# Two rounding steps taken out of the activation quantisers, Gelu released per tile, the offset of 129 moved into a column-sum bias, and no barrier between the blocks of the second feed-forward matmul

## What is computed

```python
x = x + attention(layernorm(x))
x = x + ffn(layernorm(x), w1, w2)

def _quant_weight(w):                       # ternary
    s = clip(mean(abs(w)), EPS, None)
    return clip(round(w / s), -1.0, 1.0) * s

def _quant_act(x):                          # whole numbers -128..127 per row
    scale = 127.0 / clip(max(abs(x), axis=-1, keepdims=True), EPS, None)
    return clip(round(x * scale), -128.0, 127.0) / scale

def ffn(x, w1, w2):
    h = gelu(quant_act(x) @ quant_weight(w1).T)      # 1024 -> 4096
    return quant_act(h) @ quant_weight(w2).T         # 4096 -> 1024
```

## Time and profile before

| what | us |
|---|---|
| median of 2 runs | 9029.53 (9015.09 to 9043.97) |
| profiled execution, its own time | 9021.79 |
| its span, slowest core (core 7) | 9020.3 |
| spans of the 8 cores | 8992.3 to 9020.3 |
| DVE busy | 3543.7 (39% of the span) |
| PE busy | 3752.3 (42%) |
| ACT busy | 1939.5 (22%) |
| transfers, mean over the span | 42 GB/s |

### The profile page before, as it was taken

One profiled execution on the slowest core, in us unless ns is written; L12 is line 12 of the kernel. 1 busy time (PEld: TensorE's weight loads), 2 busy tenths in 40 slices (PEclk: granted clock), 3 DMA queues, 4 the chain that ended last, 5 costly groups with the idle time before them and its releaser, 6 DMA issues.

```text
span 9020.3 us, 46886 instructions; the slowest of 8 cores (8992.3 to 9020.3 us)
## 1 busy us (share of the span) xinstructions
PE 3752.3 (42%) x13056; PEld 1408.0 (16%) x13056; DVE 3543.7 (39%) x4302; ACT 1939.5 (22%) x2197; POOL 0.2 (0%) x4
## 2 busy tenths in 40 slices
PE   3225465666653555666652003221333033025445
PEld 0000211222221211222221001110111011012222
DVE  0341323333322223333313776557555665740000
ACT  1012202555531302555421110000000000001111
POOL 0000000000000000000000000000000000000000
PEclk8666665777765755777755556655666566567778
DMA  4233100000002000000011001110111001122221
GB/s 151 98 118 96 33 0 1 9 8 10 8 26 70 21 0 3 9 9 9 9 42 49 28 31 40 56 47 10 56 56 56 27 29 56 56 63 70 75 75 54
DMA packets 204263, 374.90 MB, mean 42 GB/s; under 512 B 24345, under 2 KB 155806, under 8 KB 199922
## 3 DMA queue, kind: packets, MB, share of 16 engines
q1 hardware_dynamic: 204018, 371.92, 12.7%
HBM read 296.07 MB, written 75.76 MB: 41 GB/s over the span
## 4 chain that ended last, share of the span: by engine, by line
DVE 36%; PE 32%; ACT 15%; issue 6%; DMA 6%; SPq 3%; DVEq 1%; ACTq 0%
ACT pslab L786 8%; PE ps_F L1274 5%; DVE rlrow L830 5%; PE ps_F L1150 5%; PE pss L274 3%; PE ps_S L812 2%; PE ps_W L900 2%; PE ps_qn L760 2%; PE ps_FM L798 2%; DVE hflt L1202 2%; DVE hflt L1198 2%; DVE hflt L1200 2%; DVE htile L1197 2%; PE ps_mu L618 2%; DVE colmisc L1181 2%
## 5 line engine op out<-in xcount | busy, mean ns | idle before, releaser
L786 ACT ACTIVATE pslab<-ps_S 128x1024 bf16<-128x1024 f32 x1024 | 979.6, 1022 | 277.7 <-PE ps_S L812 275.7
L830 DVE RECIPROCAL rlrow<-ps_FM 1x512 f32<-1x512 f32 x128 | 429.0, 3352 | 1158.3 <-PE ps_FM L798 1151.3
L812 PE MATMUL ps_S<-qt,kt 65*128 65x512 bf16 x2048 | 713.6, 440 | 158.0 <-ACT pslab L786 122.5
L1213 PE MATMUL ps_trH<-s_idb,hqtm 128*128 128x128 bf16 x1024 | 129.4, 306 | 1540.8 <-DVE colmisc L1206 1439.3
L798 PE MATMUL ps_FM<-pslab,vaug 128*65 128x512 bf16 x2048 | 684.6, 422 | 170.3 <-DVE aostg L834 147.9
L1274 PE MATMUL ps_F<-hqin,w2tb 128*128 128x512 bf16 x2048 | 488.4, 400 | 556.2 <-DMA hqin<-scr_hq 337.3
L274 PE MATMUL pss<-wab,s_onescolf 128*1 128x512 f32 x512 | 310.2, 756 | 558.7 <-ACT wab L254 419.9
L1150 PE MATMUL ps_F<-w1tb,yi_fm 128*128 128x512 bf16 x2048 | 459.7, 387 | 180.0 <-DMA w1tb<-scr_w1t 179.3
L1174 ACT ACT_TABLE_LOAD x32 | 41.1, 1283 | 2120.2 <-DVE hqfm L1221 1134.7
L760 PE MATMUL ps_qn<-qsq,s_bo 128*65 128x512 f32 x256 | 233.4, 1012 | 373.3 <-DVE qt L768 323.4
L1163 DVE TENSOR_SCALAR htile<-ps_F,c1c 128x512 f32<-128x512 f32 x256 | 192.2, 751 | 447.8 <-PE ps_F L1150 436.6
(11 more groups left out here) (186 smaller groups left out, 4803.9 us busy)
## 6 DMA issues: line engine op xcount, KB each, us to landing
w1tb<-scr_w1t SPq DMA_DIRECT2D x512, 128.0 KB, 2.7
wst<-w1t SPq DMA_DIRECT2D x24, 2048.0 KB, 9.5
wst<-w2t SPq DMA_DIRECT2D x96, 512.0 KB, 3.8
xstage<-x SPq DMA_DIRECT2D x64, 512.0 KB, 4.1
scr_hq<-hqfm SPq DMA_DIRECT2D x256, 128.0 KB, 1.9
hqin<-scr_hq SPq DMA_DIRECT2D x256, 128.0 KB
rlb<-scr_rl SPq DMA_DIRECT2D x64, 256.0 KB, 3.4
scr_x<-x2asm SPq DMA_DIRECT2D x32, 512.0 KB, 2.8
```

Of the source, the lines that this page charges most:

```text
L786: sE.inc(q.activation(out=pslab[:, 1024 * (gl % 4):1024 * (gl % 4 + 1)], in_=psS[kt % 2][:], func=AF.Exp))
L812: ins = q.matmul(out=psS[kt % 2][:, 512 * s:512 * (s + 1)], lhsT=kt65[:, N * g + 128 * kt: N * g + 128 * (kt + 1)], rhs=qt65[hb][:, 1024 * ...
L830: VS(q, q.reciprocal(out=rlrow[0:1, 1024 * ph + 512 * s:1024 * ph + 512 * (s + 1)], in_=psFM[64:65, 512 * s:512 * (s + 1)]))
L1213: ins = q.transpose(out=pstr[:, 128 * j:128 * (j + 1)], in_=hqtm[:, 128 * hc:128 * (hc + 1)], identity=idb[:])
```

## The change

It makes five edits.

1. In `ln3_quant_phase` the comparison with 1.5 is gone (one DVE instruction of 128 x 1024 per tile).
2. In `ffn1_phase` the comparison with 1.5 is gone too, and the comparison with -0.5 writes straight to the bf16 tile `hqtm`, so the subtraction of 129 is gone: `hqtm` now holds values that are 129 too large.
3. For these 129, `ffn2_phase` gets a new step after `w_tern`: 256 matmuls with `w2tb` as the stationary and a column of ones as the moving operand give the column sums of `w2tb` in PSUM (`psCS`, 128 x 8). DVE multiplies them by -129 into `w2cs`. The copy of line 1284 becomes an Identity activation with `w2cs[:, dc]` as its bias. A barrier follows the new step.
4. The Gelu of tile `tt` waits only for the last `ps_F` scaling of its own tile (`bv + 4 * 7 + tt + 1`).
5. The barrier after each block of `ffn2_phase` goes; one remains after the last block. Waits take its place: SP waits for the previous block's PE steps before it loads `hqin`, and for the previous block's DVE steps before it loads `xst`; DVE waits for the stores of `y` before it writes `oasm`; PE waits for ACT and DVE from the first chunk on.

```diff
--- before.py
+++ after.py
@@ -1082,8 +1082,6 @@
                                       op=OP.subtract))
                 VS(q, q.scalar_tensor_tensor(out=yjunk[:, 0:D], in0=ytmp[:], scalar=0.5,
                                              in1=yjunk[:, 0:D], op0=OP.is_gt, op1=OP.add))
-                VS(q, q.scalar_tensor_tensor(out=yjunk[:, 0:D], in0=ytmp[:], scalar=1.5,
-                                             in1=yjunk[:, 0:D], op0=OP.is_gt, op1=OP.add))
                 VS(q, q.scalar_tensor_tensor(out=yjunk[:, 0:D], in0=ytmp[:], scalar=-0.5,
                                              in1=yjunk[:, 0:D], op0=OP.is_ge, op1=OP.add))
                 sV.inc(q.tensor_scalar(out=yib[:, D * (t % 2):D * (t % 2 + 1)], in0=yjunk[:, 0:D],
@@ -1169,7 +1167,7 @@
                 bvg = sV.n
 
                 @blk.scalar
-                def _(q, tt=tt, tgt=sV.n):
+                def _(q, tt=tt, tgt=bv + 4 * 7 + tt + 1):
                     q.wait_ge(sV.h, tgt)
                     sA.inc(q.activation(out=htile[:, HID * tt:HID * (tt + 1)],
                                         in_=htile[:, HID * tt:HID * (tt + 1)], func=AF.Gelu))
@@ -1197,12 +1195,9 @@
                         VS(q, q.tensor_tensor(out=hs, in0=hs, in1=hflt[:], op=OP.subtract))
                         VS(q, q.scalar_tensor_tensor(out=hflt[:], in0=hs, scalar=0.5,
                                                      in1=hflt[:], op0=OP.is_gt, op1=OP.add))
-                        VS(q, q.scalar_tensor_tensor(out=hflt[:], in0=hs, scalar=1.5,
-                                                     in1=hflt[:], op0=OP.is_gt, op1=OP.add))
-                        VS(q, q.scalar_tensor_tensor(out=hflt[:], in0=hs, scalar=-0.5,
+                        VS(q, q.scalar_tensor_tensor(out=hqtm[:, 1024 * sl:1024 * (sl + 1)],
+                                                     in0=hs, scalar=-0.5,
                                                      in1=hflt[:], op0=OP.is_ge, op1=OP.add))
-                        VS(q, q.tensor_scalar(out=hqtm[:, 1024 * sl:1024 * (sl + 1)], in0=hflt[:],
-                                              scalar1=129.0, scalar2=None, op0=OP.subtract))
                     sV.inc(q.tensor_copy(out=colmisc[:, 15:16], in_=colmisc[:, 7:8]))
                 for rnd in range(4):
                     @blk.tensor
@@ -1249,16 +1244,39 @@
 
         psF = st.enter_context(nc.psum_tensor(_u("ps_F2"), [128, 2 * 512], F32))
         psT2 = st.enter_context(nc.psum_tensor(_u("ps_F2T"), [128, 512], F32))
+        psCS = st.enter_context(nc.psum_tensor(_u("ps_CS"), [128, 8], F32))
         hqin = st.enter_context(nc.sbuf_tensor(_u("hqin"), [128, NC_H * 512], BF16))
         wsc = st.enter_context(nc.sbuf_tensor(_u("f2wsc"), [128, 2 * 512], F32))
+        w2cs = st.enter_context(nc.sbuf_tensor(_u("w2cs"), [128, 8], F32))
         oasm = st.enter_context(nc.sbuf_tensor(_u("oasm"), [128, 4 * 1024], F32))
         xst = st.enter_context(nc.sbuf_tensor(_u("f2xst"), [128, 2 * D], F32))
         oar = oasm[:].rearrange("p (j w) -> p j w", w=1024)
+
+        @blk.tensor
+        def _(q):
+            for m in range(NC_D):
+                for hc in range(NC_H):
+                    ins = q.matmul(out=psCS[:, m:m + 1],
+                                   lhsT=w2tb[:, 1024 * hc + 128 * m: 1024 * hc + 128 * (m + 1)],
+                                   rhs=onescolb[:, 0:1],
+                                   start=(hc == 0), stop=(hc == NC_H - 1))
+            sP.inc(ins)
+
+        @blk.vector
+        def _(q, tgt=sP.n):
+            q.wait_ge(sP.h, tgt)
+            sV.inc(q.tensor_scalar(out=w2cs[:], in0=psCS[:], scalar1=-129.0,
+                                   scalar2=None, op0=OP.mult))
+        barrier()
+        hq_free = sP.n
+        y_done = dO.n
+        st_done = sV.n
         for bl in range(8):
             bi = dI.n
 
             @blk.sync
-            def _(q, bl=bl):
+            def _(q, bl=bl, hqf=hq_free):
+                q.wait_ge(sP.h, hqf)
                 for hc in range(NC_H):
                     dI.inc(q.dma_start(out=hqin[:, 512 * hc:512 * (hc + 1)],
                                        in_=scr_hq[hc, :, 512 * bl:512 * (bl + 1)]))
@@ -1267,8 +1285,7 @@
                 @blk.tensor
                 def _(q, dc=dc, bi=bi, ba=ba):
                     q.wait_ge(dI.h, 16 * (bi + NC_H))
-                    if dc >= 2:
-                        q.wait_ge(sA.h, ba + dc - 1)
+                    q.wait_ge(sA.h, ba + max(0, dc - 1))
                     half = 512 * (dc % 2)
                     for hc in range(NC_H):
                         ins = q.matmul(out=psF[:, half:half + 512],
@@ -1281,13 +1298,14 @@
                 def _(q, dc=dc, tgt=sP.n):
                     q.wait_ge(sP.h, tgt)
                     half = 512 * (dc % 2)
-                    sA.inc(q.copy(out=wsc[:, half:half + 512], in_=psF[:, half:half + 512]))
+                    sA.inc(q.activation(out=wsc[:, half:half + 512],
+                                        in_=psF[:, half:half + 512],
+                                        func=AF.Identity, bias=w2cs[:, dc:dc + 1]))
 
                 @blk.tensor
                 def _(q, dc=dc, tgt=sA.n, bv=bv):
                     q.wait_ge(sA.h, tgt)
-                    if dc >= 1:
-                        q.wait_ge(sV.h, bv + dc)
+                    q.wait_ge(sV.h, bv + dc)
                     half = 512 * (dc % 2)
                     for j in range(4):
                         ins = q.transpose(out=psT2[:, 128 * j:128 * (j + 1)],
@@ -1296,8 +1314,10 @@
                     sP.inc(ins)
 
                 @blk.vector
-                def _(q, dc=dc, tgt=sP.n):
+                def _(q, dc=dc, tgt=sP.n, ydn=y_done):
                     q.wait_ge(sP.h, tgt)
+                    if dc == 0:
+                        q.wait_ge(dO.h, 16 * ydn)
                     sV.inc(q.tensor_copy(
                         out=oar[:, :, 128 * dc:128 * (dc + 1)],
                         in_=psT2[:].rearrange("p (j w) -> p j w", w=128)))
@@ -1305,7 +1325,8 @@
             bira, birb = dIa.n, dIb.n
 
             @blk.sync
-            def _(q, bl=bl, bvr=bvr):
+            def _(q, bl=bl, bvr=bvr, stdn=st_done):
+                q.wait_ge(sV.h, stdn)
                 for j in range(4):
                     t = 4 * bl + j
                     par = (dIa, dIb)[j % 2]
@@ -1327,7 +1348,10 @@
                                                   scalar=c2c[:, t:t + 1],
                                                   in1=xst[:, D * (j % 2):D * (j % 2 + 1)],
                                                   op0=OP.mult, op1=OP.add))
-            barrier()
+            hq_free = sP.n
+            y_done = dO.n
+            st_done = sV.n
+        barrier()
         st.close()
 
     ln3_quant_phase()
```

## The result

The changed kernel takes 8548.8 us (median of 11 runs, 8536.8 to 8598.3) against 9041.5 us (median of 10 runs, 9013.7 to 9116.1) for the kernel before. The ratio is 0.9456, with a 95% interval of 0.9429 to 0.9483: 5.4% faster. The forecast was 8565 us, 8535 to 8630.

A forecast was written before the change was run, and what follows sets the result against it. No engine was taken to bound the whole; each stage had its own limit. The terms -42.6 - 272.6 - 159 - 21 + 26 + 2 + 6 = -461 us gave 8561 or 8568, forecast 8565 us, range 8535 to 8630.

The forecast's parts named there:

- Rounding in the layernorm: Quantising layernorm: 32 DVE instructions of line 1085 go, 1.33 us each from start to start, 42.6 us gained.
- Rounding of the hidden layer: First feed-forward phase: 1.33 and 0.80 us go per slice, 128 slices, 272.6 us gained; bf16 output bounds 68 us either way.
- Gelu: First feed-forward phase: DVE's row maximum stops waiting for Gelu, 32 x (5.09 - 0.12) = 159 us gained.
- rival 3: First feed-forward phase: Gelu beside the rounding slows DVE by half, 59 us lost, 8624 us; chance 3%.
- The column sums: New step after w_tern: 256 matmuls at the transposes' pace of 0.10 us cost 26 us, bounds 13 and 113.
- The bias: Second feed-forward phase: the copy from PSUM with a per-partition operand costs 64 x 0.1 = 6 us more.
- The barrier: Second feed-forward phase: loads start 3.0 us earlier at seven boundaries, 21 us gained; store beside loads might cost 10 us.
- Gelu late: First feed-forward phase: Gelu doesn't get ahead, DVE still waits 5 us per tile, 8724 us; chance 4%.
- column sums without overlap: New column-sum step: the matmuls don't overlap at all, 87 us more, 8652 us; chance 7%.
- the clock's lower level: Feed-forward bursts: PE stays at the lower clock, up to 905 us more, 9244 us at 75% of groups; chance 2%.
- Rival 4: Second feed-forward phase: hqin loads start right after the last transposes, 154 us more gained, 8411 us; chance 1%.
- One of the signs of being wrong: Second feed-forward phase: a granted clock below 0.79 was listed among the signs that the forecast is wrong.

The follow-up runs named there:

- Experiment 4: The changed kernel with the comparison with 1.5 put back in the hidden layer's rounding only: 8717 us, the first feed-forward phase 2061.8 us.
- Experiment 3: The changed kernel with only the old wait of Gelu put back: 8730 us, the first feed-forward phase 2055.2 us instead of 1889.5.
- experiment 5: The changed kernel with four extra sets of 256 matmuls (1, 32, 64, 128 moving columns, new weight load each) behind the column sums: 8566 us.
- experiment 1: The changed kernel with the barrier after every block of the second feed-forward phase put back: 8566 us, that phase 1017.0 us instead of 1009.1.
- experiment 8: The changed kernel with two hqin buffers, four for xst, and each block's loads issued during the block before: 8254 us, second phase 686.9 us.

## Why the prediction was right

**Rounding in the layernorm.** -42.0 us measured, -42.6 forecast. The distance from start to start, 1.33 us, was the right unit; the length alone, 1.225 us, would have given 39.2.

**Rounding of the hidden layer.** Experiment 4 prices one removed instruction of the first form at 1.35 us against my 1.33. The bf16 output took the value I had chosen between the bounds, 1225 ns. What experiments 3 and 4 leave of the whole phase for the removed subtraction is 436.7 - 165.7 - 172.3 = 98.7 us, 0.77 us each against my 0.80; no run took it alone. Whole phase: -436.7, forecast -432.

**Gelu.** 162.8 us of waiting went, not 159: I had left 0.12 us per tile for a hand-over, and the profile now shows 0.0. The counter that DVE waits for has long been reached, so what is left is no more than the distance between any two instructions. Experiment 3 gives 166 us for the edit. That its cover, the three scalings of 1.73 us against 5.09 us of table load and Gelu, would just do was right, with 0.19 us to spare. Half speed beside Gelu, rival 3, didn't come.

**The column sums.** This is the term that was mis-sized: 7.0 us measured, 26 us forecast, below even my lower bound of 13. The step that failed is "the nearest are the transposes". They have 128 moving columns, and experiment 5 shows these to set the pace: 57 ns at 2.4 GHz, and the transposes' 100 ns at 1.2 GHz, against 27 ns for one column. I took the pace for that of the weight load. The row that could have told the two apart wasn't there, and the bound should have allowed for a load much shorter than the matmuls beside it. With the multiplication and the second barrier the stage grew by 8.8 us, so my 2 us for these was right (7.0 + 1.8).

**The bias.** 688 - 586 ns, taken from the group before and after, is 102 ns, times 64 is 6.5 us; forecast 6. No run took the bias alone, but -7.9 for the barrier and +6.5 make -1.4 us, and the phase moved by -1.9.

**The barrier.** Forecast -21 us; experiment 1 gives -7.9, and -14 at most by the other executions. Two steps failed. I took the gap as 3.0 us from one row, and it is 2.6 in the middle of the 56 of them. And I named the cost of the store beside the loads, "a tenth of their length would be 1.5 us per boundary", without putting it into the sum. It is real: 0.7 us of loading, and a first burst that is longer by some tenths (0.8 here, of which a part may be chance), together about half of what the gap gave.

The two misses cancel in part: the sum was 19 us too pessimistic on the column sums and 13 too hopeful on the boundary. That the forecast of 461 us stands so near to the 472 by stages is in part luck. The rivals that lay outside the range (Gelu late, column sums without overlap, the clock's lower level) didn't occur. Rival 4, loads right after the last transposes, was rightly ruled out by SP's order; what the boundary as a whole costs is shown by experiment 8, which needed second and further buffers besides the new order: 322 us. One of the signs of being wrong came, by a hair: core 7 was granted 0.78 in the second phase, the other cores 0.79 to 0.80. That is where the spell of the last section fell.

## What to carry to other kernels

Where one engine works through a chain in which each instruction waits for the last, price a removed instruction by its distance from start to start, and it holds to 2% (42.6 for 42.0 us, 1.33 for 1.35). Here a barrier was worth its gap less what the transfers it kept apart then cost each other, and it was worth little while the transfers still stood in the same order in their queue: moving the loads ahead, with a second buffer for them, gave 322 us, removing the barrier 8. Ask of a helper computation, such as a rounding correction, whether the hardware needs it at all before trimming it: one comparison fewer in each quantiser gave 214 us here (42.0 and 172.3), leaving out the whole correction another 666.

## What the runs showed that was not expected

- A matmul with a new 128 x 128 bf16 weight load and up to 32 moving columns takes 27 to 28 ns, at the 1.2 GHz level (experiment 5).
- The granted clock stayed at 0.50 through the 256 column sums, 7 us without a pause, and in experiment 5 from 7508 to 7528 us, with PE busy for 19 of 20 us; from 7530 us on, in the set of 64 columns, it was 1.00.
- The granted clock has a third value, 0.81. In one block of the second phase of the changed kernel, core 7, PE was granted 0.74 on average, where an undisturbed block of the kernel with the barrier back was granted 0.92. The first row is the changed kernel's block, of 106 us, the second a stretch inside it; the third is the block of experiment 1, core 4, 90 us:

```profile
7790.00:7896.00 106.00, 80.71 (x288) 33.44 (x288) 6.82 (x9) 15.76 (x16) 0.00 (x0) 0.74 0.03 10
7823.50:7843.00 19.50, 14.86 (x59) 6.19 (x58) 0.69 (x1) 3.94 (x4) 0.00 (x0) 0.81 0.00 0
```

```profile
7690.00:7780.00 90.00, 65.24 (x288) 29.75 (x286) 6.82 (x9) 15.76 (x16) 0.00 (x0) 0.92 0.03 12
```

Where 0.81 was granted, the matmuls of 512 columns followed each other every 0.263 us, against 0.216 at 1.00. The second phase took 1024.3 us on core 7 and 1017.6 on core 6, where the same spell came at the same place of the program, against 1003.2 to 1012.3 us on the other six. Such spells aren't bound to the changed stages: in the same execution cores 4 and 5 were granted 0.81 for 113 and 115 us from 3044 us on, far ahead of them, and in the execution of experiment 1 cores 4 to 7 had 147 to 158 us of it there. The profiled execution of the kernel before has none. The cause stays open.
